# Fused top-2 expert layer: one scatter a tile in the first pass, the boosted row turned on TensorE

## The reference, cut to what matters

```python
def _layer_norm(x, gamma, beta): ...       # over the 256 features, eps 1e-5
def expert(x, e):                          # 256 -> 512 -> 256
    return relu(x @ W1[e] + b1[e]) @ W2[e] + b2[e]

xn = (x - mean) / sqrt(var + eps)          # the block's input, before it: normalization without gain
top2 weights g0, g1 and experts e0, e1     # softmax over 8 gates, the two largest
y0 = expert(xn, e0)
y1 = expert(xn + ALPHA * y0, e1)           # ALPHA = 0.5
out = x + _layer_norm(xn + g0 * y0 + g1 * y1, gamma, beta)
```

## Time and profile before

| | |
|---|---|
| median of 3 runs | 1857.99 us (1854.67 to 1859.55) |
| the profiled execution | 1858.58 us |
| its span, first to last instruction | 1856.9 us |
| busy: PE, DVE, ACT, POOL | 1307.2, 922.5, 410.4, 454.9 us |
| mean granted TensorE clock | 0.866 of full |
| second expert layer, from its first tile to its last result | 778 to 1053 us of the span |

### The profile page before, as it was taken

One profiled execution on the slowest core, in us unless ns is written; L12 is line 12 of the kernel. 1 busy time (PEld: TensorE's weight loads), 2 busy tenths in 40 slices (PEclk: granted clock), 3 DMA queues, 4 the chain that ended last, 5 costly groups with the idle time before them and its releaser, 6 DMA issues. The chain is left out here.

```text
span 1856.9 us, 29699 instructions
## 1 busy us (share of the span) xinstructions
PE 1307.2 (70%) x9288; PEld 1038.9 (56%) x9288; DVE 922.5 (50%) x2691; ACT 410.4 (22%) x865; POOL 454.9 (24%) x466
## 2 busy tenths in 40 slices
PE   0799776886489898377694044665778898479992
PEld 0577676775356665366583024554655665368882
DVE  3577752333555564233235757775635565323333
ACT  0222201110245553011010001112345544111010
POOL 1000061221312312223222512651121432301110
PEclk9999958998699998599897576876979999789996
DMA  6000133423100000555443100000000000333315
GB/s 208 0 1 0 61 106 116 125 81 101 53 13 19 13 14 13 194 168 155 132 129 125 39 7 1 0 1 17 18 7 13 22 28 25 132 99 112 112 44 195
DMA packets 90260, 125.25 MB, mean 67 GB/s; under 512 B 11536, under 2 KB 65936, under 8 KB 89776
## 3 DMA queue, kind: packets, MB, share of 16 engines
q1 hardware_dynamic: 45152, 50.24, 8.8%
q10 hardware_dynamic: 34592, 44.41, 7.5%
q0 software_dynamic: 10416, 29.35, 4.4%
HBM read 87.09 MB, written 36.87 MB: 67 GB/s over the span
## 5 line engine op out<-in xcount | busy, mean ns | idle before, releaser
L1217 PEld LDWEIGHTS bank<-f_xT,f_up 128*128 128x128 f32 x2144 | 264.5, 198 | 9.3 <-DVE f_xT L1122 3.7
L1217 PE MATMUL bank<-f_xT,f_up 128*128 128x128 f32 x2144 | 265.4, 281 | 2.1 <-DVE f_xT L1122 2.1
L327 DVE TENSOR_REDUCE mha_nmax<-bank 128x2 f32<-128x512 f32 x256 | 170.3, 687 | 177.9 <-PE bank L446 177.8
L1226 PE MATMUL bank<-f_down,f_hT 128*128 128x256 f32 x832 | 216.3, 402 | 53.0 <-DVE f_y L1163 34.8
L994 POOL DMA_INDIRECT yout<-f_y,f_to x104 | 99.8, 960 | 486.7 <-DVE f_y L1163 221.5
L1226 PEld LDWEIGHTS bank<-f_down,f_hT 128*128 128x128 f32 x832 | 153.8, 196 | 94.7 <-DVE f_y L1163 47.6
L446 PE MATMUL bank<-mha_k,mha_q 32*128 32x256 f32 x1024 | 153.6, 419 | 49.6 <-DVE mha_nmax L327 36.2
L265 ACT ACTIVATE mha_probT<-bank 128x512 f32<-128x512 f32 x256 | 139.2, 598 | 166.4 <-PE bank L454 166.4
L454 PE MATMUL bank<-mha_q_top,mha_k 32*128 32x256 f32 x1024 | 148.9, 409 | 2.5 <-DVE mha_q_top L336 2.0
L446 PEld LDWEIGHTS bank<-mha_k,mha_q 32*128 32x128 f32 x1024 | 92.4, 193 | 91.6 <-DVE mha_nmax L327 56.7
L1059 ACT ACTIVATE f_hT<-bank,f_b 128x128 f32<-128x128 f32 x148 | 46.2, 363 | 354.5 <-PE bank L1217 347.5
(11 more groups left out here) (278 smaller groups left out, 2361.8 us busy)
## 6 DMA issues: line engine op xcount, KB each, us to landing
f_up<-in_W ACTq DMA_DIRECT2D x32, 512.0 KB, 4.5
f_xt<-rows SPq DMA_DIRECT2D x108, 136.0 KB, 2.2
f_down<-in_W ACTq DMA_DIRECT2D x24, 512.0 KB, 5.5
f_took<-yout SPq DMA_DIRECT2D x48, 256.0 KB, 5.7
mha_ctxT<-in_ctxT SPq DMA_DIRECT2D x16, 256.0 KB, 2.7
f_up<-in_V ACTq DMA_DIRECT2D x8, 512.0 KB, 4.2
f_down<-in_Wout ACTq DMA_DIRECT2D x8, 512.0 KB, 6.3
f_meta<-rows ACTq DMA_DIRECT2D x20, 128.0 KB, 2.1
```

What stands on the lines that cost most here:

```text
L327: vector.tensor_reduce(nmax[:, p, :, at], ps_s[n % 2][:, :].rearrange("p (k s) -> p k s", s=S), AX.X, ALU.min).then_inc(max_ready, 1)
L1217: ins = pe.matmul(into, up[q][i][:, c, m * P:(m + 1) * P], xT[:, c, :], start=c == 0, stop=c == DC - 1)
L1226: ins = pe.matmul(ps_y[:, 0:D], hT[:, m, :], down[q][:, m, :], start=m == 0, stop=m == HC - 1)
```

## The change

The two choices of a token are now both laid down by the routing. `G.rows[1]` becomes twice as long: a slot of the second pass is a pair of rows. The routing scatters `xn`, with token, shares and target, to the first row of the pair (so `scatter` issues two indirect DMAs a tile instead of one in the second layer), and pass 0 scatters its `y` straight to the second row. `meta`, `row2`, the second scatter and their waits are gone. Pass 1 loads the pair, 528 columns, in one DMA. TensorE makes the boosted row by accumulating, for each half, the turned `xn` (moving operand: identity) and the turned `y` (moving operand: half the identity) in the bank: 4 matmuls in place of 2 transposes. DVE in pass 1 also makes `base` = share0 * y0 + xn when the tile arrives, and `z` = share1 * y + base at its end, and `z` is what GpSimd scatters, to one row a token. `fuse` then loads one row a token and needs no L906. The softmax shares are computed in the routing (`weigh` on ACT, four small instructions more a batch in `place` on DVE). GpSimd adds beta to X during pass 1 and the last addition to X is DVE's.

Some edits concern all three expert layers. Rows have 264 columns instead of 272. SP issues one padding DMA instead of four, ACT four, GpSimd three (in the second layer also those of pass 1, inside pass 0, one at each expert's start). Each engine reads the loop bounds of a pass at its start: 8 register loads before the first tile instead of 16 in the second layer, the other 8 between the passes. The shares of the first and fourth layer are computed after the first tile is turned.

```diff
-            for k in range(2 if self.joint else 1):
-                pool.indirect_dma_start(self.G.rows[0][:, :], bass.IndirectOffsetOnAxis(self.slots[:, t, k:k + 1], 0),
+            for k in range(2):
+                rows = self.G.rows[0 if self.joint or k == 0 else 1]
+                pool.indirect_dma_start(rows[:, :], bass.IndirectOffsetOnAxis(self.slots[:, t, k:k + 1], 0),
                                         self.src[:, t, :], None).then_inc(self.scattered, 16)
...
+            def add(b):
+                x = X[:, TPB * b:TPB * (b + 1), :]
+                vector.wait_ge(shifted_x, b + 1)
+                vector.wait_ge(gained, b + 1)
+                vector.tensor_tensor(x, x, took[:, TPB * b:TPB * (b + 1), 1, :], ALU.add)
...
-            ends = [ends_of(sync, p) for p in range(len(passes))]
-            sync.wait_ge(rt.scattered, rt.all_scattered)
             for p, at in enumerate(passes):
                 prime(sync, at.x_landed)
+                first = rows_of(sync, p, 0)
+                ends = ends_of(sync, p)
                 if p:
-                    sync.wait_ge(passes[0].sent, 16 + 16 * count)
+                    sync.wait_ge(passes[0].stored, 16 + 16 * count)
                     sync.sem_inc(went_on, 1)
+                else:
+                    sync.wait_ge(rt.scattered, rt.all_scattered)
...
-                        sync.dma_start(xt[:, :], rows(j)).then_inc(at.x_landed, 16)
-
-                count = each_expert(ends[p], tiles)
+                        sync.dma_start(xt[:, 0:width[p]], rows(j)).then_inc(at.x_landed, 16)
...
+                if p:
+                    pool.wait_ge(affine_landed, 16)
+
                 def tiles(e, lo, hi):
+                    if BOOST and p == 0:
+                        rt.pad(pool, 1, pads[1], (e,))
+                    if p:
+                        x = X[:, TPB * e:TPB * (e + 1), :]
+                        pool.tensor_tensor(x, x, gamma_beta[:, 1, :].unsqueeze(1).to_broadcast([P, TPB, D]),
+                                           ALU.add).then_inc(shifted_x, 1)
+                    away, sent = (G.rows[1], y[:, :]) if BOOST and p == 0 else (G.yout, z[:, :] if p else y[:, 0:D])
                     with pool.Fori(lo, hi) as j:
                         pool.wait_ge(at.y_ready, PRIMED + j + 1)
                         pool.sem_inc(went_on, 1)
-                        pool.indirect_dma_start(G.yout[:, :], bass.IndirectOffsetOnAxis(to[:, 0:1], 0),
-                                                y[:, :], None).then_inc(at.stored, 16)
-                        if BOOST and p == 0:
-                            pool.wait_ge(at.boosted, PRIMED + j + 1)
-                            pool.sem_inc(went_on, 1)
-                            pool.indirect_dma_start(G.rows[1][:, :], bass.IndirectOffsetOnAxis(to[:, 1:2], 0),
-                                                    row2[:, :], None).then_inc(at.sent, 16)
-
-                each_expert(ends[p], tiles)
...
+                    if p:
+                        based(j)
+                    marked(j)
+
+                def marked(j):
+                    vector.tensor_copy(marks[:, bass.ds(j, 1), :].rearrange("p o k -> p (o k)"), xt[:, TOK:TOK + 4]).then_inc(at.x_free, 1)
+
+                def based(j):
+
+                    if not isinstance(j, int):
+                        vector.wait_ge(at.y_ready, PRIMED + j - 1)
+                    vector.scalar_tensor_tensor(out=base[:, bass.ds(j % 2, 1), :].rearrange("p o d -> p (o d)"),
+                                                in0=xt[:, ROW:ROW + D], scalar=xt[:, SHARE:SHARE + 1], in1=xt[:, 0:D],
+                                                op0=ALU.mult, op1=ALU.add).then_inc(at.based, 1)
...
-                            vector.tensor_copy(to[:, 0:1], mark(0))
-                            if p == 0:
-                                vector.wait_ge(at.sent, 16 + 16 * j)
-                                vector.tensor_copy(to[:, 1:2], mark(1))
-                                vector.tensor_scalar(row2[:, TOK:TOK + 1], mark(0), 1.0, None, ALU.add)
+                            vector.tensor_copy(to[:, 0:1], mark(0 if p else 1))
                         vector.wait_ge(at.y_done, PRIMED + j + 1)
                         if GLU:
-                            vector.tensor_copy(y[:, :], ps_y[:, 0:D]).then_inc(at.y_ready, 1)
+                            vector.tensor_copy(y[:, 0:D], ps_y[:, 0:D]).then_inc(at.y_ready, 1)
+                        elif p:
+                            vector.tensor_tensor(y[:, 0:D], ps_y[:, 0:D], b2[:, e, :], ALU.add).then_inc(at.summed, 1)
+                            vector.wait_ge(at.summed, PRIMED + j + 1)
+                            vector.wait_ge(at.based, PRIMED + j + 1)
+                            vector.scalar_tensor_tensor(out=z[:, :], in0=y[:, 0:D], scalar=mark(3),
+                                                        in1=base[:, bass.ds(j % 2, 1), :].rearrange("p o d -> p (o d)"),
+                                                        op0=ALU.mult, op1=ALU.add).then_inc(at.y_ready, 1)
                         else:
-                            vector.tensor_tensor(y[:, :], ps_y[:, 0:D], b2[:, e, :], ALU.add).then_inc(at.y_ready, 1)
-                        if BOOST and p == 0:
-                            vector.wait_ge(at.meta_landed, 16 * j + 16)
-                            vector.wait_ge(at.y_ready, PRIMED + j + 1)
-                            vector.scalar_tensor_tensor(out=row2[:, 0:D], in0=y[:, :], scalar=0.5, in1=meta[:, :],
-                                                        op0=ALU.mult, op1=ALU.add).then_inc(at.boosted, 1)
-
-                each_expert(ends[p], expert)
+                            vector.tensor_tensor(y[:, 0:D], ps_y[:, 0:D], b2[:, e, :], ALU.add).then_inc(at.y_ready, 1)
...
-                        ins = pe.transpose(ps_t[:, c * R:(c + 1) * R], xt[:, c * P:(c + 1) * P], G.const("ident"))
+                        to = ps_t[:, c * R:(c + 1) * R]
+                        if p:
+                            pe.matmul(to, xt[:, c * P:(c + 1) * P], G.const("ident"), start=True, stop=False)
+                            ins = pe.matmul(to, xt[:, ROW + c * P:ROW + (c + 1) * P], half[:, :], start=False, stop=True)
+                        else:
+                            ins = pe.transpose(to, xt[:, c * P:(c + 1) * P], G.const("ident"))
```

178 lines of the change are left out of this document (97 added, 81 removed).

## The result

The changed kernel takes **1812.0 us** (median of 4 runs, 1808.8 to 1814.3) where the kernel before takes 1858.6 beside it. The ratio is 0.9752, its 95% interval 0.9731 to 0.9773: 47 us faster. The forecast was 1816 in a range of 1800 to 1836.

A forecast was written before the change was run, and what follows sets the result against it. No engine is busy over 70%; scatters bound the passes, registers the second layer's start, DVE `fuse`. Sum: -4.5 - 8 + 1.5 - 25.5 + 2 + 12 - 20 = -42.5 from 1858.58, that is 1816 us, range 1800 to 1836.

The forecast's parts named there:

- the starts: Expert layers' first loads: 8 us gained in the second layer, 4.5 for first and fourth together, from fewer paddings and register loads.
- `fuse`: End of the second expert layer: without L906, DVE's chain falls to 3.5 us a batch; 20 us gained.
- Pass 0: Second expert layer's first pass: without second scatter, row2 steps and meta load, 5.94 a step becomes 4.60; 25.5 us gained.
- The 0.08 that I added for paddings: Pass 0's step: 0.08 us added because the transfer of GpSimd's padding at each expert's start does not vanish.
- Between the passes: Pass 0's end to pass 1's start: eight more register loads (4.8), a faster load of rows, cold matmuls; 2 us lost.
- Pass 1: Second expert layer's second pass: z adds 0.54 to the scatter's path, disturbance 0.1; step 5.16, 12 us lost.
- Rival (a): Pass 1: the load into xt becomes the bound, 6.0 a tile; 15 us more, 1831; chance 0.15.
- Rival (b): Pass 0: period stays at 5.3, set by weights and paddings, not the second scatter; 13 us more, 1829; chance 0.10.
- (c): Better than the sum: fewer collisions in both passes, all 3.3 of SP's in both outer layers; 12 less, 1804; chance 0.10.
- (d): Pass 1: TensorE's clock drops to 1.2 GHz throughout; 75 us more, 1891, slower than before; chance 0.04.
- (e): Pass 1's turning: an ordinary fp32 matmul costs four times a transpose's 0.11; TensorE 5.3 a tile, 1819; chance 0.01.
- Attention of six batches: Before the second expert layer: extra scatters covered, DVE's small steps of 0.8 a batch partly exposed; 1.5 us lost.

The follow-up runs named there:

- small weights: The changed kernel with second-expert-layer weight loads after the first three experts' cut from 512 KB to 64 KB: pass 0 77.9 us, pass 1 95.2.
- the old split: The changed kernel with each layer's first-region paddings issued as before, four by SyncE, four by ScalarE, none by GpSimd: 1853.8 us.
- weights held back: The changed kernel with pass 1's weight loads issued only after the last scatter of the tile before has landed: 1849.9 us, ratio 0.9891.
- half of the load: The changed kernel with pass 1's load bringing only each row's first half (132 KB instead of 264): pass 1 94.7 us, whole 1798.5.

## Why the prediction was right, and which terms were off

The time was right within 4 us, and the large terms by their mechanism. That the sum came so near is luck: against the profiled 44.3 us, stretches that came out shorter than forecast (the starts, `fuse`, attention, the border behind `fuse`) make up 15 us, and those that came out longer (both passes, the stretch between them, the third layer) 13. Pass 0 was the second scatter's place in the chain and nothing else: putting it back gives 5.96. `fuse` was DVE's four additions for the most part (15.0 of 21.6).

**Pass 0, 22.2 instead of 25.5.** The price of 4.52 was taken from pass 1 of before. But five experts' weights are issued within pass 1 and seven within pass 0 (ScalarE's queue shows them, from 771.94 to 847.63), and one costs 1.8 us by the run with small weights. Two more are 3.7 us, and 4.60 against 4.78 is 3.4. That is an estimate which fits: what weights cost in pass 1 of the kernel before was not measured, and in the changed pass 1 small weights gained only 1.3. The 0.08 that I added for paddings has no support: with small weights and all paddings in place the first twelve steps are 3.87 to 4.00.

**The starts, -20.1 instead of -12.5.** The second layer's 10.4 was just over my upper bound. I took three of SyncE's paddings as worth 3.3 a layer at most and gave the first and fourth layer 4.5 together, for fear that the scatters would be late next. They are not: the old split costs 4.0, 2.5 and 3.0 up to the first load. The other term that I had too small is the load's own time. Going out ahead of the weights was priced at up to 1.5 for the first and fourth layer and at nothing for the second. It takes 2.2 us to the first turned tile of the fourth layer instead of 5.6, and 2.1 instead of 3.6 in the second. The first layer shows only 1.8 because its first padding stands 2.3 later than before (277.43 against 275.16), for a reason ahead of it that I did not look for; counted from there to the next attention it is 4.1, and 4.7 by the run.

**Between the passes, +6.9 instead of +2.** The registers were priced right (4.8; 5.7 to 6.5 by the run), but I had the scatter land 3.0 behind its start, and SyncE's first register load behind the wait for it is at 868.9, 5.0 behind it. ScalarE's weights leave at 862.83, one microsecond ahead of that scatter. I counted this earlier issue only as a gain for the load of rows; with small weights, or with the weights held back, the scatter is there after 2.5, and the stretch is 3.4 and 3.1 shorter. The rest is TensorE: from the first turning to the first `y` it is 9.9 instead of 6.7. The four turning matmuls are eight records in place of two. At the low clock, 0.21 apart, they take 2.07 us at 877.23, where they take 1.0 in pass 1, and they come twice before that `y`. In the kernel before, the second turning was at full clock already: its records are 0.11 apart from 913.7 on, 4.3 behind its first; here from 886.96 on, 9.7 behind.

**Pass 1, +15.3 instead of +12.** The quiet steps that the scatter sets are 4.6 (eleven of them with half of the load) and were forecast at 4.79, near by two errors that partly cancel: from the end of `y` to the end of `z` it is 0.30 + 0.48 for the 0.54 taken from L1167 (`z` starts 0.2 later behind its `y`; why is open), and the scatter lands in 2.5 for the 3.0 that I had. What was mis-sized is the 0.1 for everything else: it is 0.6, in the eleven other steps. Rival (a) is half true: the load's cycle is 5.07, not 4.6 (load with its issue 2.87 for 3.0, turning until DVE copies 1.3 for 0.6, the copies with `base` 0.9 for 1.0). The turning is the term that failed, by a misreading: 16 records were taken for 16 matmuls, while they are eight. So the two added matmuls, with the two transposes that became ordinary ones, cost TensorE six records more a tile, 0.66 us and not 0.24, and all of it stands in the load's cycle. That an `xT` turned in fewer records would bring pass 1 nearer to its 4.6 was not tested. The load's cycle is the bound in one part of the steps and the scatter in the other, which is why no edit of one chain moved the pass by more than 3 us, and two together shortened it by 4.6. It did not reach the rival's 6.0 a tile.

Rival (b) is refuted as a cause of its own, though weights do cost pass 0 12.9 us; (c) and (d) did not occur. On (e), the prediction's reading of the rows and the price it argued against are both off: an ordinary matmul is two records 0.11 apart, 0.22 in all, against 0.11 for a transpose. That is twice the transpose's price, where the prediction took the two to cost the same and set that against a factor of four. Attention of six batches was priced at +1.5 and shows -1.7. Five kernels with the same attention spread from 275.5 to 277.9 us on this chip up to the first padding and the kernel before has 277.5, so no cost of the small steps shows, and no gain either.

## What to carry to other kernels

When a price is taken from a neighbouring loop, count what else runs in each of the two: here two more loads of weights are about the size of the error. Count records of the trace against calls in the program before taking a price for one call: here that was a factor of two, and it stood in a chain that became a bound. When two chains of a loop are within a tenth of each other, shortening one alone gave nothing here; they had to be shortened together, and TensorE's own work and the transfers that disturb both come next. Register loads and descriptor issues in front of a stage's first load are on the path in full: move them ahead of the last wait, and before adding a wait to a queue, list what stands behind it.
